# Moving the weight loads and butterflies of the Hadamard layer into the attention before it, and its weight products to the front

## The reference, cut to what matters

```python
x = x + _L1_attn_ref(xn, ...) + _L1_ffn_ref(xn, ...)

def _L1_ffn_ref(input, SU_ug, SU_dp, Wscale_ug, Wscale_dp, W_up, W_gate, W_down):
    x = fwht(x * SU_ug) / SCALE                       # 256 wide
    x_up = x @ W_up.T * (Wscale_ug[:INTER] * SCALE)   # 256 -> 1024
    x_gate = x @ W_gate.T * (Wscale_ug[INTER:] * SCALE)
    x = jax.nn.silu(x_gate) * x_up
    x = fwht(x * SU_dp) / SCALE                       # 1024 wide
    x = x @ W_down.T * (Wscale_dp * SCALE)
```

## Time and profile before

| what | us |
|---|---|
| median of three runs (2175.12 to 2186.74) | 2183.26 |
| the profiled execution: its time | 2191.86 |
| the profiled execution: its span | 2190.1 |
| a1, from its first projection to the end | 391.9 to 597.9 |
| f1, block | 598.1 to 711.5 |
| in it: up to the first gate product | 598.1 to 626.1 |

### The profile page before, as it was taken

How to read it: one execution, slowest core, us unless ns; L and a number is a source line. 1 busy time by engine, 2 the same in 40 slices (tenths; PEclk the granted TensorE clock), 3 DMA queues, 4 the chain that set the end, 5 groups by cost and what they waited for, 6 DMA issues and landing times. The chain is left out here.

```text
span 2190.1 us, 45878 instructions
## 1 busy us (share of the span) xinstructions
PE 1938.6 (89%) x16932; PEld 1223.8 (56%) x16932; DVE 1323.2 (60%) x2490; ACT 973.0 (44%) x2372; POOL 1050.7 (48%) x2230
## 2 busy tenths in 40 slices
PE   7879897987779889747999999999999999999888
PEld 5412564432234453434777777777777777777753
DVE  2634554885535447355777777677777777777531
ACT  3365232104311321134556665666556655666430
POOL 0530122000120014207888887788878887888720
PEclk7899998977989989778999999999999999999899
DMA  5033323000020110112322222222222222222200
GB/s 146 1 125 132 93 47 69 23 0 1 3 98 0 55 37 29 31 37 51 59 50 61 60 52 51 61 61 61 56 51 61 60 52 50 64 61 50 38 10 19
DMA packets 217273, 113.09 MB, mean 52 GB/s; under 512 B 138432, under 2 KB 197472, under 8 KB 216672
## 3 DMA queue, kind: packets, MB, share of 16 engines
q1 hardware_dynamic: 212976, 105.06, 19.1%
q0 software_dynamic: 4080, 5.15, 1.5%
HBM read 81.79 MB, written 31.54 MB: 52 GB/s over the span
## 5 line engine op out<-in xcount | busy, mean ns | idle before, releaser
L2483 POOL TENSOR_TENSOR a_term<-a_z,a_l 32x14 f32<-32x14 f32 (+6 forms) x896 | 344.4, 384 | 70.3
L2487 POOL TENSOR_TENSOR a_z<-a_z,a_term 32x14 f32<-32x14 f32 (+6 forms) x896 | 340.4, 380 | 70.2
L2034 PE MATMUL ps<-all_xn,a_w_qkv 128*128 128x512 f32 x512 | 249.1, 613 | 3.3 <-DVE a_at L2533 3.3
L2513 DVE SCALAR_TENSOR_TENSOR a_qkv<-a_raw,a_taps,a_qkv 128x1024 f32<-128x1024 f32 x192 | 246.9, 1286 | 6.2
L1592 POOL TENSOR_TENSOR all_x<-all_x,f_part_out 128x512 f32<-128x512 f32 x32 | 45.9, 1469 | 228.9 <-DVE f_part_out L1565 228.9
L2044 PE MATMUL ps<-a_w_z,all_xn 128*128 128x256 f32 x512 | 126.5, 392 | 17.1 <-ACT a_zs L2310 17.1
L2034 PEld LDWEIGHTS ps<-all_xn,a_w_qkv 128*128 128x128 f32 x512 | 89.9, 194 | 75.1 <-issue 68.5
L2233 PE MATMUL ps<-a_out_t,a_w_out 128*128 128x256 f32 x512 | 129.3, 396 | 1.9 <-ACT a_out_t L2385 1.7
L838 POOL DMA_INDIRECT f_sums<-a_y,a_xs x23 | 36.1, 1568 | 194.8 <-ACT a_y L788 191.9
L2306 ACT ACTIVATE a_raw<-ps 128x512 f32<-128x512 f32 x128 | 76.5, 598 | 116.1 <-PE ps L2034 115.4
L2044 PEld LDWEIGHTS ps<-a_w_z,all_xn 128*128 128x128 f32 x512 | 96.0, 195 | 29.8 <-ACT a_zs L2310 17.5
(11 more groups left out here) (325 smaller groups left out, 4412.3 us busy)
## 6 DMA issues: line engine op xcount, KB each, us to landing
a_gc_rows<-a_g_dram SPq DMA_DIRECT2D x64, 256.0 KB, 4.8
a_v_dram<-a_v SPq DMA_DIRECT2D x64, 256.0 KB
a_w<-in_f_w SPq DMA_DIRECT2D x24, 512.0 KB, 6.2
a_w_qkv<-in_a_w SPq DMA_DIRECT2D x16, 512.0 KB, 3.9
a_t_dram<-a_z SPq DMA_DIRECT2D x512, 8.0 KB
f_index_in<-in_f_index SPq DMA_DIRECT2D x2, 2144.0 KB, 10.8
a_w_z<-in_a_w SPq DMA_DIRECT2D x16, 256.0 KB, 2.8
a_w_out<-in_a_wo SPq DMA_DIRECT2D x16, 256.0 KB, 3.1
```

Of the source, the lines that this page charges most:

```text
L2034: mm = pe.matmul(ps[:, to, :], w_qkv[:, k, mt * P:(mt + 1) * P], xn[:, k, b * T:(b + 1) * T], start=k == 0, stop=k == KC - 1)
L2483: pool.tensor_tensor(term[:, 0:j, j + 1:], z[:, 0:j, j:j + 1].broadcast_to([HP, j, n]), rows[:, j:j + 1, j + 1:].broadcast_to([HP, j, n]), ...
L2487: pool.tensor_tensor(z[:, 0:j, j + 1:], z[:, 0:j, j + 1:], term[:, 0:j, j + 1:], ALU.add).then_inc(sub_step, 1)
L2513: dve.scalar_tensor_tensor(to, rows, tap, to, ALU.mult, ALU.add).then_inc(conv_ready if j == TAPS - 1 else conv_step, 1)
```

## The change

The buffers and loads of f1's weights move into a class, `HadamardWeights`, which is made before a1 starts. Its `load` (all nine transfers, those of the tables of signs and scales too) is issued by SyncE within a1's block, once `k_psum` has reached NI // 2 = 4. Its `transform` (the six butterfly instructions) stands in GpSimd's list of a1 in front of the eight multiplications. In f1, TensorE's four weight products and ScalarE's four copies of them now stand in front of those of `mixed`. `look.load` is then SyncE's first work in f1. The numbers of instructions stay the same.

```diff
-def alibi_attention(nc, ps, d, x, xn, norm):
+def alibi_attention(nc, ps, d, x, xn, norm, then):
...
             @block.sync
             def _(sp):
                 Stage.clear_stale(sp)
+                sp.wait_ge(k_psum, NI // 2)
+                then.load(sp)
...
             @block.gpsimd
             def _(pool):
+                then.transform(pool)
                 for i in range(NI):
                     pool.wait_ge(mixed_ready, i + 1)
...
+class HadamardWeights:
+    def load(self, sp):
+        d = self.d
+        for to, of in ((self.su_ug, "f1_su_ug"), (self.had, "hadamard"), (self.su_dp, "f1_su_dp"),
+                       (self.sc_up, "f1_sc_up"), (self.sc_gate, "f1_sc_gate"), (self.sc_dp, "f1_sc_dp")):
+            sp.dma_start(to[:, :], d[of]).then_inc(self.small, 16)
+        sp.dma_start(self.raw[:, :, :], d["f1_w_down"].rearrange("(f p) n -> p f n", p=P)).then_inc(self.down_loaded, 16)
+        for to, of in ((self.gate, "f1_w_gate"), (self.up, "f1_w_up")):
+            sp.dma_start(to[:, :, :], d[of].rearrange("(k p) n -> p k n", p=P)).then_inc(self.w_loaded, 16)
+
+    def transform(self, pool):
+
+        pool.wait_ge(self.down_loaded, 16)
+        for n, (of, to) in enumerate(((self.raw, self.mid), (self.mid, self.raw), (self.raw, self.mid))):
+            if n:
+                pool.wait_ge(self.w_step, n)
+            r = 1 << n
+            a = of[:, :, :].rearrange("p (q two r) n -> p q two (r n)", two=2, r=r)
+            o = to[:, :, :].rearrange("p (q two r) n -> p q two (r n)", two=2, r=r)
+            pool.tensor_tensor(o[:, :, 0, :], a[:, :, 0, :], a[:, :, 1, :], ALU.add)
+            pool.tensor_tensor(o[:, :, 1, :], a[:, :, 0, :], a[:, :, 1, :], ALU.subtract).then_inc(self.w_step, 1)
...
+        @block.sync
+        def _(sp):
+            look.load(sp)
+            Stage.clear_stale(sp)
+
+        @block.tensor
+        def _(pe):
+            pe.wait_ge(small, 6 * 16)
+            pe.wait_ge(w_step, 3)
+            for q in range(4):
+                pe.matmul(ps[:, 4 + q, :], had[:, :],
+                          w_mid[:, 2 * q:2 * q + 2, :].rearrange("p f n -> p (f n)"),
+                          start=True, stop=True).then_inc(w_psum, 1)
+            for k in range(KC):
+                pe.wait_ge(mixed_ready, k + 1)
...
+            pe.wait_ge(w_loaded, 2 * 16)
+            pe.wait_ge(xh_ready, KC * B)
...
         if "a1" in stages:
-            alibi_attention(nc, ps, d, x, xn, norm("n1"))
-        if "f1" in stages:
-            hadamard_layer(nc, ps, d, x, xn, looked_up)
+            with Stage(nc, "f1") as h:
+                weights = HadamardWeights(h, d)
+                alibi_attention(nc, ps, d, x, xn, norm("n1"), weights)
+                hadamard_layer(nc, h, ps, d, x, xn, looked_up, weights)
```

More of the change, by code:

```diff
@@ L1654, in _, with __init__ @@
                         dve.tensor_tensor(part, part, ps[:, 4 + b * KC + m, :], ALU.add).then_inc(added, 1)
-def hadamard_layer(nc, ps, d, x, xn, looked_up):
+class HadamardWeights:
+    INTER = 1024
+    def __init__(self, s, d):
+        FT = self.INTER // P
+        self.d = d
+        self.gate, self.up = s.buf("w_gate", [P, KC, self.INTER]), s.buf("w_up", [P, KC, self.INTER])
+        self.raw, self.mid = s.buf("w_raw", [P, FT, C]), s.buf("w_mid", [P, FT, C])
+        self.had = s.buf("had", [P, P])
+        self.su_ug, self.su_dp = s.buf("su_ug", [P, KC]), s.buf("su_dp", [P, FT])
+        self.sc_up, self.sc_gate, self.sc_dp = (
+            s.buf("sc_up", [P, FT]), s.buf("sc_gate", [P, FT]), s.buf("sc_dp", [P, KC]))
+        self.small, self.w_loaded, self.down_loaded = s.sem("small"), s.sem("w_loaded"), s.sem("down_loaded")
+        self.w_step = s.sem("w_step")
+    def load(self, sp):
[16 more added lines that the diff above has]
+            pool.tensor_tensor(o[:, :, 1, :], a[:, :, 0, :], a[:, :, 1, :], ALU.subtract).then_inc(self.w_step, 1)
@@ L1662, in hadamard_layer @@
+def hadamard_layer(nc, s, ps, d, x, xn, looked_up, weights):
     INTER = 1024
     FT = INTER // P
[L1664 to L1726, removed]
[L1727 to L1793 removed]
@@ new lines, in hadamard_layer @@
+    w_gate, w_up, w_mid, had = weights.gate, weights.up, weights.mid, weights.had
+    su_ug, su_dp, sc_up, sc_gate, sc_dp = weights.su_ug, weights.su_dp, weights.sc_up, weights.sc_gate, weights.sc_dp
+    small, w_loaded, w_step = weights.small, weights.w_loaded, weights.w_step
+    w_down = s.buf("w_down", [P, FT, C])
+    sc_both = s.buf("sc_both", [P, FT])
+    signed, mixed = s.buf("signed", [P, KC, N]), s.buf("mixed", [P, KC, N])
+    xh = s.buf("xh", [P, KC, N])
+    act_h, gated = s.buf("act_h", [P, 2, T]), s.buf("gated", [P, 4, T])
```

134 lines of the change are left out of this document (72 added, 62 removed).

## The result

The changed kernel takes 2155.7 us in the median of six runs (2152.21 to 2165.49) against 2180.7 for the kernel before in the same measurement: ratio 0.9897, 95% interval 0.9878 to 0.9916, so 18 to 27 us less. (The ratio is estimated from all the runs, so it is not the quotient of the two medians, which is 0.9885.) Timed a second time, on other runs, it came to 2168.1 against 2188.1: ratio 0.9916, 0.9896 to 0.9936, 14 to 23 us less. The forecast of 20.0 us less (0.9908 of 2183.26) lies in both intervals.

What follows compares the result with a forecast made beforehand. TensorE was taken to bound f1's body, and waits for tables and butterflies its opening. 0 in a1 and -20.0 in f1 took 2191.86 to 2171.9 us; carrying over 8.6 us above the median gave 2163.3, range 2153 to 2177.

Steps and rivals of the forecast that it cites:

- The removed waits: Opening of f1: without the wait for the butterflies, the gate loop starts at 606.1 instead of 626.12, 20.0 us less.
- VectorE hidden behind the weight products: Opening of f1: `mixed` halves ready at 600.9 and 602.1, TensorE reaching them at 601.6 and 603.3 after the weight products.
- ScalarE's last copy uncovered: End of f1's opening: the first gate product now waits for the last copy to `xh`, 0.2 + 0.6 + 0.2 us.
- The index list: f1: issued first, it lands after 7.8 us, before VectorE's first multiplication at 611.9, costing nothing; late-list rival, chance 0.02.
- the worse bound: f1: index list taking 13.8 us from issue to landing, as behind 3 MB of weights; even then no cost.
- The butterflies in a1: a1, 437 to 451 us: GpSimd's butterflies cost VectorE zero; rival that they hold it back 14.1 us, chance 0.05.
- the other bound: a1: 14.1 us lost if VectorE and GpSimd exclude each other for the whole of the butterflies.
- The low clock in the opening: Rival in f1's opening: both product groups run at the low clock, 5.0 us lost, giving 2168.3 us; chance 0.11.
- The transfer to the median: Whole kernel: the profiled execution's 8.6 us over the median carries over, turning 2171.9 into 2163.3 us.
- The total: Whole kernel: 0 in a1, -20.0 in f1, nothing behind; 2163.3 us, 0.92% less.

Runs made afterwards that it cites:

- the repeats: Both kernels unaltered, profiled again in single executions, the changed one twice and the one before twice; the changed kernel timed again has ratio 0.9916 to the kernel before.
- e1: Changed kernel with the products of `mixed` put first again in f1, weight products behind them; ratio 0.9925 to the kernel before.
- e6: Changed kernel with SyncE held in f1 until the last copy to `xh` before it issues the index list; 2165.57 us in one execution, no ratio.
- e4: Changed kernel with the butterflies in a1 done five times over, thirty instructions instead of six; ratio 0.9930 to the kernel before.
- e2: Changed kernel with loads kept in a1, but butterflies back at the start of f1 and `mixed` first again; ratio 0.9953 to the kernel before.

## Why the prediction was right

*The removed waits.* 20.0 us predicted for the opening, 19.88 measured in the first pair of profiles (27.99 to 8.11), and 19.95 and 20.5 between the repeats. The two groups of eight entries followed each other at 592.90 - 589.39 = 3.51 and, up to the last slot, 3.4 us (3.44 each predicted). TensorE started 0.23 us behind SyncE, for which 0.07 had been taken, and that is most of the 0.14 us that the opening is longer than the 7.97 of the sum.

*VectorE hidden behind the weight products.* Right: the first half of `mixed` was done near 591.9, TensorE came to it at 592.90. Its counterfactual was under-sized: without the weight products in front, the prediction had TensorE only idle until then, and e1 showed 1.5 us of low clock besides.

*ScalarE's last copy uncovered.* Right: 0.78 us idle in front of the loop. The chain of slot, copy and handover back was put at 0.2 + 0.6 + 0.2 us and took 0.94: the copy ran from 596.53 to 597.13, the gate product followed 0.14 later.

*The index list.* The predicted 7.8 us was 7.5, and the wait cost nothing. But the step left something out: VectorE waits for all three transfers of `look.load`, and the third was issued 0.87 us after the first. The cover was therefore 603.12 - (590.03 + 7.5) = 5.6 us and not 6, and at the worse bound of 13.8 us it would have been 0.7 us short (590.03 + 13.8 = 603.83) and not just enough. e6 showed the price of this.

*The butterflies in a1.* Taken at zero against a bound of 14.1 us. e4 settles it for VectorE: five times the butterflies left its durations and a1's first phase as they were. The row it rested on (L1565, one SBUF tensor and PSUM) was the right one. e2 shows that the other bound was no fancy: beside the same six butterflies VectorE's five instructions in front of the products took 10.6 us longer, and the butterflies themselves 2.6. The rule of the Trainium skill (SBUF — State Buffer, section Who interferes with whom) is borne out in both halves: beside PSUM readers no duration changed, and the product of scales, with two SBUF inputs, waited for as long as a whole butterfly lasts. The later butterflies were stretched too, to 2.66 to 3.33 us, so it seems that the two engines took turns in coming second. One caution for the reader of the prediction: L178 and the signs read only one SBUF tensor, and both were slowed (to 1.82 us from 0.83, to 2.90 from 0.75). By these rows the number of SBUF inputs is not the whole test; the instructions that went untouched all read PSUM.

The moved work came earlier than forecast, at 428.35 to 442.48 and not near 437 to 451: a1 began 6.8 us earlier in this profile, and its fourth key projection came 34.7 us behind the first projection instead of 36.6. From the first issue to the first butterfly it took 8.47 us, of 2.75 + 5.7 predicted. The prediction also named VectorE alone as what bounds a1 there; from 432 to 452 TensorE was busy 19.89 us of 20 as well. Nothing rests on that, since no duration changed.

*The low clock in the opening.* Given 0.11; it didn't happen in any of the three profiles of the changed kernel, with 1.3 us of idle time at the barrier. It did happen in e1, after 4.01 us.

*The transfer to the median.* The profiled execution before was 8.6 us over its median, and the prediction took this difference over. That is not shown: the profiled execution of the changed kernel was 9.8 us over its own median. What is shown is that the lines changed are not the source of such differences, since n1, in front of them, begins anywhere from 367.2 to 384.0 us. Comparing the two spans alone (26.4 us) would have overrated the change by 6.5 us.

*The total.* The first median of the changed kernel, 2155.7, is 7.6 us below the 2163.3 forecast: 2.6 because the kernel before had a median of 2180.7 in this measurement and not 2183.26, the rest because the gain came out at 22.5 us by the ratio (25.0 by the medians). The profiles account for 19.9 of it. The second measurement has 18.4 us by the ratio. So the opening is predicted closely and by its mechanism, while the total is known only to some 4 us to each side, and that 20.0 us lies in both intervals says no more than that.

## What to carry to other kernels

Work that only prepares weights belongs in the idle queue of an earlier stage, but what it costs there depends on what its neighbour reads: the same six GpSimd instructions were free beside VectorE instructions that take PSUM and one SBUF tensor, and cost 10.6 us of VectorE's time beside ones that work on SBUF alone. The order behind a barrier is to be chosen anew once a wait has gone: "weight products first" lost 4.65 us while the butterflies stood on the path, and gained 3.2 us afterwards, almost half of it by keeping TensorE's clock up. And where stages vary by 5 to 10 us between executions, a gain is read as the length of its own stretch, not as the difference of two spans, and two stretches are compared at the same distance from the stage's start and at the same clock.

## What the runs showed of the hardware that was not expected

- GpSimd and VectorE slow each other by turns: a scaling of 1024 elements on VectorE went from 0.75 to 2.86 us beside butterflies, a tensor operation of two SBUF inputs from 1.22 to 3.30, one of eight elements from 0.17 to 2.34, and the butterflies from 2.34 up to 3.33.
- Beside VectorE instructions that read PSUM, 69.8 us of GpSimd showed no effect on their durations: 64 maxima, 40 of them beside it, at 425/826/1227 ns with and without.
- On GpSimd the scaling of 1024 elements takes 2.84 us and a tensor operation with two inputs 2.34, so the one with fewer inputs is the slower.
- Some three megabytes of DMA into SBUF (146 GB/s over 20 us) and the butterflies beside them left VectorE's busy time in the same stretch at 19.52 of 20 us, as without them.
